# Reordering the ScalarE and VectorE streams of a Strassen-Winograd linear layer, with its first weight difference stored once and fewer statistics passes

## The reference, cut to what matters

```python
# x: (8, 512, 2048) float32; per batch one adapter of rank 16
h = x @ base_weight.T + base_bias + (x @ A[id].T) @ B[id].T        # (8, 512, 2048)
query = h @ Wq.T; scores = (query @ Wr.T) @ (aux_keys @ Wr.T).T / sqrt(48) + log_rel
top8 of 512 -> softmax of query @ keys / 8 + log_rel -> sum of values -> @ Wvd.T @ Wvu.T = aux_out
var = jnp.var(h, axis=-1)                                           # needs sum(h), sum(h*h) per token
norm_var = log1p(var) / (mean(log1p(var)) + 1e-6)                   # the mean is over all tokens
u = clip(0.5 * norm_var + 2.5 * sigmoid(gelu(h @ Wu1.T + bu1) @ Wu2.T + bu2), 0, 5)
out = x + h + gate(u) * aux_out
```

## Time and profile before

| | us |
|---|---|
| median of 3 runs | 1991.33 (1990.09 to 1993.81) |
| the profiled execution, its own time | 1987.83 |
| its span, first to last instruction | 1986.0 |
| mean granted clock of TensorE | 0.993 |
| second part starts, us of the span | 1385.9 |

### The profile page before, as it was taken

How to read it: one execution, slowest core, us unless ns; L and a number is a source line. 1 busy time by engine, 2 the same in 40 slices (tenths; PEclk the granted TensorE clock), 3 DMA queues, 4 the chain that set the end, 5 groups by cost and what they waited for, 6 DMA issues and landing times.

```text
span 1986.0 us, 24922 instructions
## 1 busy us (share of the span) xinstructions
PE 1938.8 (98%) x8682; PEld 1579.0 (80%) x8682; DVE 1256.6 (63%) x1653; ACT 696.4 (35%) x1057; POOL 388.2 (20%) x275
## 2 busy tenths in 40 slices
PE   8999999999999999999999999999999999999997
PEld 6777877888888888888888887777788888888885
DVE  5675688555457846546773743677566677666675
ACT  3322333333234333323333422445343233323322
POOL 2210123020012202002210100120343322233231
PEclk9989999999999999999999999999999999999999
DMA  7656777552367745146774425666887777777795
GB/s 268 222 190 237 257 261 265 168 174 74 117 203 236 226 150 177 56 147 210 234 226 135 165 85 180 229 196 223 282 276 260 248 231 237 228 240 239 236 379 220
DMA packets 196354, 416.56 MB, mean 210 GB/s; under 512 B 26821, under 2 KB 27845, under 8 KB 196103
## 3 DMA queue, kind: packets, MB, share of 16 engines
q1 hardware_dynamic: 150726, 325.83, 50.7%
q10 hardware_dynamic: 45504, 89.15, 11.8%
HBM read 317.37 MB, written 97.52 MB: 209 GB/s over the span
## 4 chain that ended last, share of the span: by engine, by line
PE 82%; DVE 6%; issue 4%; DMA 2%; ACT 2%; SPq 1%; POOL 1%; ACTq 0%; DVEq 0%; POOLq 0%
PE bank L1772 17%; PE bank L1773 17%; PE bank L1774 17%; PE bank L1810 6%; PE bank L1811 6%; PE bank L1812 6%; PE bank L1917 1%; PE bank L1919 1%; PE bank L1918 1%; PE bank L1828 1%; PE bank L1827 1%; PE bank L1712 1%; PE bank L1713 1%; PE bank L1700 1%; DVE sums L1338 1%
## 5 line engine op out<-in xcount | busy, mean ns | idle before, releaser
L1772 PE MATMUL bank<-xop,wsp 128*128 128x512 f32 x1792 | 710.5, 396 | 16.4 <-DVE wsp L1229 8.3
L1773 PE MATMUL bank<-xop,wsp 128*128 128x512 f32 x1792 | 701.8, 392 | 0.0
L1774 PE MATMUL bank<-xop,wsp 128*128 128x512 f32 x1792 | 701.0, 391 | 0.0
L1772 PEld LDWEIGHTS bank<-xop,wsp 128*128 128x128 f32 x1792 | 338.6, 189 | 101.0 <-DVE xop L1229 9.0
L1773 PEld LDWEIGHTS bank<-xop,wsp 128*128 128x128 f32 x1792 | 338.6, 189 | 74.2 <-issue 3.8
L1774 PEld LDWEIGHTS bank<-xop,wsp 128*128 128x128 f32 x1792 | 338.1, 189 | 72.5
L1229 DVE TENSOR_TENSOR wsp<-wraw,wsp 128x1024 fp32r<-128x1024 f32 x184 | 236.9, 1288 | 122.1 <-ACT wsp L852 121.9
L852 ACT ACTIVATE wsp<-wraw 128x1024 fp32r<-128x1024 f32 x184 | 193.9, 1054 | 207.2 <-PE bank L1774 172.7
L833 POOL TENSOR_TENSOR r_h<-r_h,r_x 128x512 f32<-128x512 f32 x128 | 175.3, 1370 | 370.7 <-DMA r_h<-h_dram 327.9
L939 ACT ACTIVATE stage<-stage 128x512 f32<-128x512 f32 x128 | 80.9, 632 | 403.3 <-DVE stage L1324 403.3
L1338 DVE TENSOR_TENSOR sums<-sums,stage 128x1024 f32<-128x1024 f32 x116 | 154.4, 1331 | 90.4 <-ACT stage L939 90.3
(11 more groups left out here) (169 smaller groups left out, 1953.3 us busy)
## 6 DMA issues: line engine op xcount, KB each, us to landing
wraw<-in_w SPq DMA_DIRECT2D x131, 512.0 KB, 3.8
xraw<-in_x SPq DMA_DIRECT2D x248, 256.0 KB, 4.3
wraw<-t_dram SPq DMA_DIRECT2D x80, 512.0 KB, 3.6
h_dram<-stage ACTq DMA_DIRECT2D x128, 256.0 KB, 3.9
hraw<-h_dram SPq DMA_DIRECT2D x128, 256.0 KB, 4.1
r_x<-in_x SPq DMA_DIRECT2D x128, 256.0 KB, 4.4
r_h<-h_dram SPq DMA_DIRECT2D x128, 256.0 KB, 3.5
out<-o_st ACTq DMA_DIRECT2D x96, 256.0 KB, 3.9
```

Of the source, the lines that this page charges most:

```text
L1772: pe.matmul(ps, wsp[:, slot, 0, f], x_hi(i), start=(k == 0), stop=False)
L1773: pe.matmul(ps, wsp[:, slot, 0, f], x_lo(i), start=False, stop=False)
L1774: last = pe.matmul(ps, wsp[:, slot, 1, f], x_hi(i), start=False, stop=(k == HT - 1))
```

## The change

Six edits go together. ACT's `square_and_store` is taken one step later and stands after the next weight split. DVE's `add_sums` keeps its tile but moves from the start of a step to just before `finish`. T1 is stored once, from `t_res`, right after it is made (`store_t1`, at ACT's steps 2 to 7, 10 and 12), and M5 of pair 0 loads it back like the later pairs; `make_t1_again` is gone, and `make_t2` waits for the landed store. T4 is made two tiles earlier. Statistics have two segments a pair (8 in all, the last one at step 5 of the second part, with what follows it moved to later steps). `lora_b` stands after k = 5 in place of k = 3.

```diff
-        T4_AT = {18 + o: o for o in range(HT)}
+        T4_AT = {16 + o: o for o in range(HT)}
         T3_AT = {M7 * HT - 3 + o: o for o in range(HT)}
-        T1B_AT = {M5 * HT - 3 + o: o for o in range(HT)}
...
-        SEGMENT = {M2: 0, M4: 1, M5: 1, M3: 2}
-        STATS_AT = {(M6, 1): 0, (M3, 2): 1, (M1, 2): 2}
+        STATS_AT = {(M3, 3): 0, (M1, 3): -1}
+        def segment(p, q):
+            return 2 * p + (q in (M2, M3))
...
+            def store_t1(o):
+                act.wait_ge(t_ready, t_count("t1", o))
+                act.dma_start(t_dram[T1, o], t_res[:, o, :]).then_inc(t_moved[o], 16)
...
                 if g + 2 < TILES:
                     split_w_hi(g + 2)
+                if g > 1 and tile_of(g - 2)[1] in H_PRODUCTS:
+                    square_and_store(g - 2)
+                if g - 1 in T1_AT:
+                    store_t1(T1_AT[g - 1])
...
-                if g > 0 and tile_of(g - 1)[1] in H_PRODUCTS:
-                    square_and_store(g - 1)
+            square_and_store(TILES - 2)
+            split_wu_hi(7)
             square_and_store(TILES - 1)
-            split_wu_hi(7)
...
             def make_t2(o):
                 wait_w(dve, "t2", o)
-                dve.wait_ge(t_ready, t_count("t1", o))
+                dve.wait_ge(t_moved[o], 32)
...
-            def make_t1_again(o):
...
-                if g > 1 and tile_of(g - 2)[1] in H_PRODUCTS:
-                    add_sums(g - 2)
                 if g + 2 < TILES:
                     split_w_lo(g + 2)
...
+                if g > 1 and tile_of(g - 2)[1] in H_PRODUCTS:
+                    add_sums(g - 2)
                 if g > 0 and tile_of(g - 1)[1] in H_PRODUCTS:
                     finish(g - 1)
...
+                    if k == 5 and g > 0 and tile_of(g - 1)[1] in H_PRODUCTS:
+                        lora_b(g - 1)
                     if k == 3:
-                        if g > 0 and tile_of(g - 1)[1] in H_PRODUCTS:
-                            lora_b(g - 1)
...
-                elif k == 1:
-                    stats_pass(3 * NPAIR - 1)
-                elif k == 8:
+                elif k == 5:
+                    stats_pass(NB - 1)
+                elif k == 13:
```

More of the change, by code:

```diff
@@ L227, in bass_adaln_ffn @@
         xr_in = [sem(f"xr_in{i}") for i in range(NXR)]
-        tb_in = [sem(f"tb_in{i}") for i in range(HT)]
+        t_moved = [sem(f"t_moved{i}") for i in range(HT)]
         a_in = sem("a_in")
@@ L366, in bass_adaln_ffn @@
                 continue
-            early = p == 0 and q in (M7, M5)
+            early = p == 0 and q == M7
             entries.append((g - 3 if early else g - 2, 0, "tile", g))
@@ L383, in is_stored @@
             kind, g = entries[n][2:4]
-            return kind == "t4" or kind == "tile" and g < PAIR and tile_of(g)[1] in (M7, M5)
+            return kind == "t4" or kind == "tile" and g < PAIR and tile_of(g)[1] == M7
         def wait_stored(eng, kind, g):
@@ L522, in load_w @@
                         sp.wait_ge(wl_ready, og + 1)
-                        if p == 0 and q in (M7, M5):
+                        if p == 0 and q == M7:
                             wait_stored(sp, "tile", og)
@@ L553, in load_w @@
                         src = w[o, :, 0:WT]
[L554 removed]
+                    elif q == M3:
                         src = w[HT + o, :, WT:2 * WT]
                     else:
[L557 removed]
+                        if q == M5:
+                            sp.wait_ge(t_moved[o], 32)
+                        elif p == 0:
                             wait_stored(sp, "t4", o)
@@ L873, in split_w_hi @@
                         act.wait_ge(t_ready, t_count("t3", o))
-                    if p == 0 and q == M5:
-                        act.wait_ge(t_ready, t_count("t1b", o))
                     src = w_raw("tile", g)
                 to_hi(wsp[:, g % NW, 0, :], src).then_inc(wh_ready, 1)
-                if p == 0 and q in (M7, M5):
-                    act.dma_start(t_dram[T3 if q == M7 else T1, o], src).then_inc(t_out[W_PLACE["tile", g] % NWR], 16)
+                if p == 0 and q == M7:
+                    act.dma_start(t_dram[T3, o], src).then_inc(t_out[W_PLACE["tile", g] % NWR], 16)
+            def store_t1(o):
+                act.wait_ge(t_ready, t_count("t1", o))
+                act.dma_start(t_dram[T1, o], t_res[:, o, :]).then_inc(t_moved[o], 16)
             def store_t4(o):
@@ L1173, in _ @@
                     split_wvu_hi((k - 3) // 2)
-                if c == 0 and k == 6:
+                if c == 0 and k == 9:
                     act.wait_ge(mstep, 4)
@@ L1426, in _ @@
                         split_x_lo(pp, pq, k)
-                if (q, o - 1) in STATS_AT:
-                    seg = 3 * p + STATS_AT[q, o - 1] - (3 if q == M1 else 0)
-                    if seg >= 0:
-                        copy_stats(seg)
+                if stats_at(p, q, o - 1) is not None:
+                    copy_stats(stats_at(p, q, o - 1))
                 if g == LAST + M5 * HT + 1:
@@ L1791, in _ @@
                             router_factor()
-                    if k == 5 and (q, o) in STATS_AT:
-                        seg = 3 * p + STATS_AT[q, o] - (3 if q == M1 else 0)
-                        if seg >= 0:
-                            stats_pass(seg)
+                    if k == 5 and stats_at(p, q, o) is not None:
+                        stats_pass(stats_at(p, q, o))
             lora_b(TILES - 1)
```

48 lines of the change are left out of this document (20 added, 28 removed).

## The result

The changed kernel takes 1975.53 us (median of 4 runs, 1970.52 to 1976.41); the kernel before took 1990.71 beside it (1988.92 to 1993.81). The ratio is 0.9917, with a 95% interval of 0.9899 to 0.9935: 15 us or 0.8% faster. The profiled execution took 1974.81 us with a span of 1973.0, that is 13.0 less than before's span of 1986.0. The forecast sum was 26.3.

The account below looks back on a forecast made before the run. PE, busy 98% of the span, was taken as the bound, with waits in pair 0 and at the second part's start. 7.2 + 9.5 + 8.8 + 0.8 + 4.5 - 4.5 = 26.3 us gave 1963 us, range 1953 to 1979.

Parts of the forecast that it names:

- The rival of transfers: Pair 0 becomes bound by transfers: late loads, M6's wait partly stays; gain only 10 to 18 us, 1970 to 1979; chance 0.17.
- the early term: Loss from T1's stores in the first 100 us: 4.5 us in the forecast, 8 to 12 under the rival of transfers.
- two signs of being wrong: PE's waits in the first 110 us growing by more than 8 us, or M6 keeping its 3.7 us wait.
- Statistics: Four fewer statistics passes on PE, 1.8 us each, save 7.2 us (6.8 to 7.4).
- T1 not made again: In M5 and M3 of pair 0, DVE loses eight instructions and the whole excess goes: 9.5 us saved.
- Sums later, squares not waited for: In M2 and M6 of pair 0, shorter DVE steps make x ready earlier: 8.8 us saved (3 to 9.8).
- T4 two tiles earlier: At M7 of pair 0, T4 loads at tiles 24 and 25 go: 0.8 us saved; tile 17's delay costs nothing, at worst 2.
- T1's stores: Eight 512 KB stores move into the first 100 us and delay loads in M1 and M2: 4.5 us lost (0 to 11.8).
- The second part's start: Waits for last `finish` and statistics and slow clock go, a new 2.5 us `query7_pass(0)` wait comes: 4.5 us saved (2 to 7).
- Pair 3's M3: A sixth `combine` wait, 1.3 us in pair 3 at M5's end, counted as no gain: later sums eat k = 5's 1.4 us.

Follow-up runs that it names:

- the statistics alone: The kernel before with two statistics segments a pair at their later places, nothing else changed; median 1979.71 us, ratio 0.9939 to the kernel before.
- the second profile: The changed kernel run and profiled once more, nothing changed; median 1973.36 us, ratio 0.9922 to the kernel before.
- the query later: The changed kernel with the first eight `query7_pass` of the last batch one step later; median 1970.51 us, ratio 0.9915 to the kernel before.
- all together: The changed kernel with T4 at 18, T1 made again, ACT's Wu and h splits before the square in the last two tiles, query one step later; 1957.51 us.
- The kernel with the adapter matmul at k = 3: The changed kernel with T4 at 18, T1 made again and `lora_b` back at k = 3; median 1963.97 us, ratio 0.9863 to the kernel before.

## Why the prediction was right, and where it was not

The time, 1975.5, lies in the range (1953 to 1979) and the kernel is faster, as forecast, but it is 12.5 us above the point and outside the forecast's own 1957 to 1970. The rival of transfers (1970 to 1979) names the time better than the forecast does, and half of its reason: the loss came through transfers, but by the round trip of a place in the weight buffers, not by full queues. In M6 the DMA share is 0.65, and the early term stayed at 4.5, below this rival's 8 to 12. Neither of the two signs of being wrong came: PE's waits in the first 110 us grew by 2.3 (10.4 to 12.7), and M6's 3.7 became 0.7. By the steps of the sum:

- **Statistics, -7.2: right.** 43.77 against 45.62 in three pairs is 1.85 each; with pair 0's, 7.4.
- **T1 not made again, -9.5: right in size, the cause not the one named.** M5 and M3 of pair 0 lost 8.36 and 1.17. But with T1 made again, in the new order and at k = 5, M5 is 45.55 to 45.91 as well. With T1 stored, k = 5 and the old order it is 45.55 too. With k = 5 either edit suffices (T1 stored with k = 3 and the old order was not run); the prediction gave the whole sum to one because it costed them apart. The same 7 us stand in the order's account.
- **Sums later, squares not waited for, -8.8 in M2 and M6: right in kind, 6.2 in size.** From the statistics alone to the same in the new order, M2 gains 0.5, M6 5.7. M2's 2.04 us of excess mostly stayed (50.44 against pair 1's 49.05), which the prediction had given away with x's wait. In the changed kernel the term doesn't show, since the next one takes it.
- **T4 two tiles earlier, -0.8: the step that failed.** The prediction wrote that the load behind T4's first store delays DVE by some 4 us and that "this costs nothing, at worst 2 us", and that M7's wait "stays". The delay was 5.2. In the kernels in the new order, M6 and M7 together average 103.7 us with T4 at 16 (101.6 to 106.4, six profiles, two of them of the changed kernel) and 96.7 with T4 at 18 (96.3 to 97.3, four): **+7.0 us**; in the changed kernel it is two waits and the matmuls at 0.43 us behind each. The slack was taken as two tiles, 11 us. It was 3.3: without the wait the weight of tile 20 would have been split from 133.41 (138.61 - 5.20) to 134.62, and PE was ready for it at 137.89 (139.97 - 2.08). 5.2 - 3.3 is 1.9, and the wait is 2.08. "Two tiles ahead" is the order of the program; DVE was itself late in it. And the chain of places was followed for one link only. With T4 at 16 each link of it, store, landing, load, `make_t4`, stands later against PE, to the end of M7.
- **T1's stores, +4.5: inside its bounds, mis-sized.** The profiled execution shows 4.5 by luck. Its first tile alone is 1.4 us longer than before's (14.62 against 13.22) and ends at 22.4 us, before the first T1 store is issued at 28.2: PE's matmuls stay longer at the spacing of 0.43 us. Windows of before and of the changed kernel:

```profile
14.00:16.00 2.00, 2.00 (x10) 1.44 (x10) 1.00 (x2) 1.06 (x1) 0.00 (x0) 1.00 0.62 142
...
14.00:16.00 2.00, 2.00 (x6) 1.30 (x6) 1.18 (x2) 0.87 (x1) 0.00 (x0) 1.00 0.54 176
```

This first tile takes 12.3 to 14.6 us over all profiles, with the stores and without. M1 and M2 average 105.2 us in the seven profiles with the stores (102.4 to 106.9) and 103.1 in the six without (102.0 to 104.2); from tile 2 on, 86.1 and 84.1. So the stores cost some 2.1 us. As this buys nothing in M5 at k = 5, storing T1 was a small loss. The Trainium skill (DMA: Bandwidth & Descriptors, Issuing engines are not separate DMA queues) says that DMAs run on the same 16 DMA engines and interleave, whichever engine issued them. By this rule the term is above zero; the two averages agree, though the two ranges overlap.
- **The second part's start, -4.5: failed, it was +0.2** (-2.7 in the second profile). The mechanism was right: statistics no longer waited for, one new wait of `query7_pass(0)` for `h_sp`. It was sized 2.5 and is 4.51. The last `finish` ends 3.9 us after the part's start (at 1376.55 against 1372.67), 1.6 later than forecast, and makes PE wait 1.71 where the sum had 0.25, so PE comes to the query 1.9 us later than forecast too (1381.20, 8.5 after the part's start, against 6.7). What lengthens the second wait is that ACT's split follows the store's issue by 7.7 us (1384.30 - 1376.57), where the earlier trace rows gave 5.4 (1394.65 - 1389.21): the store landed late, and the last section shows beside what. In the ten profiles with the statistics at step 5 and the query at its old place this wait is 4.0 to 4.5 us where the store landed latest (five), 2.9 in two, and 1.3 to 2.2 in the three where it landed as before. A wait of 4.5 then brings the slow clock, 9 matmuls in 3.69 us, which the sum had taken off. With the query one step later the part is 5.5 to 6.0 us shorter than before's.
- **Pair 3's M3, 0: it gained 1.3**, k = 5 mostly (1.7 in the experiment).

Measured in the one profile: -7.4 (passes), -9.5 (M5, M3), +0.2 (M6 and M7 without pair 0's pass), +4.5, +0.2, -1.3 and +0.3 elsewhere in pair 3 are the 13.0 us; of the +4.5, 1.4 was gone in the first tile. The forecast had -9.6 for M2, M6 and M7 and -4.5 for the second part; the two misses, with 1.3 won in pair 3, make the 13 us between 26.3 and 13.0.

Open is why M6 and M7 scatter by 5 us between kernels that differ elsewhere. Whether M7's remaining 5.3 us would go with one more weight place was not tried.

## What to carry to other kernels

When a block is moved earlier, follow the buffer places that it passes through to the end of the chain, not to the first link: each is a store, its landing and a load, and an engine that waits at one link is late at all of them. Cost edits that cure the same wait together: with two cures the second is worth nothing, and if it has a price of its own, it is a loss. When an input leaves the critical path by going to DRAM and back, give it the slack of its slowest round trip in the trace; a step of program order is cheaper than any transfer.

## What the runs showed of the hardware

The same 256 KB store of h landed after 2.0 us in the kernel before and after 4.3 in the changed one, with no other load or store in flight beside it; in the second there were two packets of the queues that the profile calls "instruction". DMA views of 1389 to 1392 us of before and of 1376 to 1381.5 of the changed kernel (GB/s in 40 slices):

```profile
GB/s 0 0 0 0 0 0 0 0 0 0 0 0 0 191 300 382 355 382 382 382 410 410 219 82 0 0 0 0 0 0 0 0 0 0 0 0 0 0 0 0
...
q10 hardware_dynamic: 144, 0.26, 23.2%
...
h_dram<-stage ACTq DMA_DIRECT2D x1, 256.0 KB, 2.0
```

```profile
GB/s 0 0 0 0 0 0 0 0 0 0 253 492 357 343 313 90 15 30 0 15 30 30 0 15 0 15 0 15 15 30 30 0 0 0 0 0 0 0 0 0
...
q10 hardware_dynamic: 144, 0.26, 13.2%
q8 instruction: 1, 0.02, 2.0%
q14 instruction: 1, 0.01, 0.9%
...
h_dram<-stage ACTq DMA_DIRECT2D x1, 256.0 KB, 4.3
```

In the second nearly all of the store is moved as fast as in the first; then 18 of its 144 packets, in two runs of nine, trickle at 15 to 30 GB/s for 2 us, and the store counts as landed only behind the last. The two instruction packets are what they stand behind. By their share of 16 engines' 5.5 us they took 1.76 and 0.79 us (in the trace 1.73 and 0.76). The small one ends at 1378.290 us and the first run of nine starts at 1378.287; the large one ends at 1379.313 and the second run starts at 1379.299. All 13 profiles fit. From this store's issue to SP's issue of the load of `r_h` it is 2.5 to 2.6 us in the five where no such packet starts before the store's own packets are through, 3.2 to 3.3 in the three with an 8 KB one alone, and 4.3 to 4.8 in the five with a 16 KB one. Two profiles of one program, the changed kernel, have 4.8 and 3.2; no experiment moved these packets. So part of what the second part won or lost in any single profile above is this luck, also with the query later and with all together, whose stores met no 16 KB packet.

Unexpected too is how far apart a kernel's executions lie: 1964 to 1975 us with the query later, against 1957.2 to 1959.5 with all together. The kernel with the adapter matmul at k = 3, whose T4 is also at 18, has 1959.4 to 1966.7, so T4's chain alone doesn't explain it, and what does isn't shown.
